# Turning the identity matrix in TensorE's waits, and moving slot and clear work on VectorE, in a cross-attention and mixture-of-experts kernel

## What is computed

```python
x = x + attention(layernorm(x), ctx, mask, W_q, W_k, W_v, W_o, b_o)
xf = layernorm(x)
probs = softmax(xf @ Wr)
topk_probs, topk_experts = top_k(probs, 2)
for e in range(8):
    gate = sum(where(topk_experts == e, topk_probs, 0))
    vals, idx = top_k(where(any(topk_experts == e), gate, -inf), 1120)
    h = relu(xf[idx] @ W1[e]) @ W2[e]
    y = y.at[idx].add(where(isfinite(vals), vals, 0)[:, None] * h)
return x + y
```

## Time and profile before

| | |
|---|---|
| median of 3 runs | 2058.97 us (2055.81 to 2060.05) |
| the profiled execution's own time | 2061.44 us |
| its span, first to last instruction | 2059.7 us |
| mean granted TensorE clock | 0.977 of full |
| busy: PE / DVE / ACT / POOL | 95% / 49% / 35% / 23% |
| chain that ended last: PE, of it L1714 | 69%, 64% |
| PE busy in the stretch 578.3 to 622.7 us | 20.07 of 44.40 us |

### The profile page before, as it was taken

One profiled execution on the slowest core, in us unless ns is written; L12 is line 12 of the kernel. 1 busy time (PEld: TensorE's weight loads), 2 busy tenths in 40 slices (PEclk: granted clock), 3 DMA queues, 4 the chain that ended last, 5 costly groups with the idle time before them and its releaser, 6 DMA issues.

```text
span 2059.7 us, 30182 instructions
## 1 busy us (share of the span) xinstructions
PE 1954.4 (95%) x11419; PEld 1733.6 (84%) x11419; DVE 1002.4 (49%) x2471; ACT 719.4 (35%) x1928; POOL 477.0 (23%) x560
## 2 busy tenths in 40 slices
PE   5799999999849999999999999999999999999997
PEld 4688888888638889989889888888998988889996
DVE  4678888887676353334133413432343353236221
ACT  4566776666414132123112311321132132115111
POOL 2445555455510021011001100111101011112101
PEclk9899999999959999999999999999999999999999
DMA  7011332211144144124112411341142144116102
GB/s 210 19 52 53 87 87 74 66 53 36 54 142 144 16 118 123 15 52 145 45 15 57 139 46 16 105 120 31 28 141 73 16 112 113 31 21 162 32 5 27
DMA packets 96316, 148.40 MB, mean 72 GB/s; under 512 B 8608, under 2 KB 50096, under 8 KB 96160
## 3 DMA queue, kind: packets, MB, share of 16 engines
q1 hardware_dynamic: 80288, 109.41, 16.9%
q0 software_dynamic: 15872, 36.71, 9.9%
HBM read 110.70 MB, written 35.39 MB: 71 GB/s over the span
## 4 chain that ended last, share of the span: by engine, by line
PE 69%; DVE 1%; issue 1%; POOL 0%; POOLq 0%; ACT 0%; DVEq 0%
PE psH L1714 33%; PE psY L1714 31%; PE psY L1753 2%; PE psX L1728 1%; PE psI L1776 1%; DVE w_lo L1129 0%; PE psI L1766 0%; POOL out_dram L1498 0%; POOLq L1410 0%; DVE hT_lo L1688 0%; PE psI L1782 0%; DVE moves L1564 0%; DVE onehot L1572 0%; DVE slot_tile L1649 0%; DVE ys L1647 0%
## 5 line engine op out<-in xcount | busy, mean ns | idle before, releaser
L1688 DVE SCALAR_TENSOR_TENSOR hT_lo<-psH,hT_hi 128x384 fp32r<-128x384 f32 (+1 forms) x384 | 210.0, 547 | 867.3 <-ACT hT_hi L1528 527.9
L1528 ACT ACTIVATE hT_hi<-psH 128x384 fp32r<-128x384 f32 (+1 forms) x384 | 185.4, 483 | 1063.3 <-PE psH L1714 1063.3
L1714 PE MATMUL psH<-xgT_hi,w_hi 128*128 128x256 f32 (+3 forms) x1536 | 477.7, 311 | 9.6 <-issue 8.8
L1714 PE MATMUL psH<-xgT_hi,w_lo 128*128 128x256 f32 (+3 forms) x1536 | 476.6, 310 | 2.1 <-issue 2.1
L1714 PE MATMUL psH<-xgT_lo,w_hi 128*128 128x256 f32 (+3 forms) x1536 | 475.3, 309 | 1.7 <-issue 1.7
L1714 PE MATMUL psY<-w_hi,hT_hi 128*128 128x512 f32 (+1 forms) x921 | 371.7, 404 | 0.0
L1714 PE MATMUL psY<-w_lo,hT_hi 128*128 128x512 f32 (+1 forms) x921 | 362.7, 394 | 1.1 <-issue 1.1
L1714 PE MATMUL psY<-w_hi,hT_lo 128*128 128x512 f32 (+1 forms) x921 | 362.3, 393 | 0.0
L1714 PEld LDWEIGHTS psH<-xgT_hi,w_hi 128*128 128x128 f32 x1536 | 291.5, 190 | 35.3 <-issue 18.5
L1714 PEld LDWEIGHTS psH<-xgT_lo,w_hi 128*128 128x128 f32 x1536 | 291.7, 190 | 14.9
L1714 PEld LDWEIGHTS psH<-xgT_hi,w_lo 128*128 128x128 f32 x1536 | 291.4, 190 | 4.1 <-issue 4.1
(11 more groups left out here) (229 smaller groups left out, 2870.2 us busy)
## 6 DMA issues: line engine op xcount, KB each, us to landing
stage<-in_L_ffn_W_dram SPq DMA_DIRECT2D x128, 512.0 KB, 4.5
x_sb<-in_x_dram SPq DMA_DIRECT2D x8, 896.0 KB, 5.6
x_res<-in_x_dram SPq DMA_DIRECT2D x8, 896.0 KB, 5.6
out_dram<-x_res SPq DMA_DIRECT2D x8, 896.0 KB, 4.8
xn_rows<-xn SPq DMA_DIRECT2D x8, 896.0 KB, 4.8
c_sb<-in_ctx_dram SPq DMA_DIRECT2D x8, 384.0 KB, 6.2
c_sb<-in_ctx_dram SPq DMA_DIRECT2D x32, 96.0 KB, 5.8
out_dram<-zrow SPq DMA_DIRECT2D x9, 256.0 KB, 4.2
```

The lines of the kernel that those rows point to most:

```text
L1528: h = nc.scalar.activation(hT[0][:, f % 2, 0:m], psH[f % 2][:, 0:m], ACT.Relu)
L1688: h = nc.vector.scalar_tensor_tensor(out=hT[1][:, f % 2, 0:m], in0=psH[f % 2][:, 0:m], scalar=0.0, in1=f32(hT[0][:, f % 2, 0:m]), op0=ALU. ...
L1714: mm = nc.tensor.matmul(out, stationary(a, c), moving(b, c), start=first and c == chunks[0] and j == 0, stop=last and c == chunks[-1] and ...
```

## The change

A helper `turn_over` transposes the 128x128 identity matrix into a PSUM bank that is free at the time. Nobody reads the result, and the turns wait for nothing and raise no semaphore. They are put ahead of TensorE's waits: 42 in the prologue, 16 after it, 25 in `PE_END`, 40 in the router and 80 at the start of the experts, 203 in all. On VectorE, `place(slice(1, E))` goes from behind `gid` to behind the gates, ahead of the first `h_lo`. The clears of the two `psH` banks go from behind it to the end of `early_slots`, ahead of the wait for the last early product.

```diff
+def turn_over(nc, T, bank, times):
+    for _ in range(times):
+        nc.tensor.transpose(bank[:, 0:128], T["ident"][:], T["ident"][:])
...
-PE_END = order("t-3 o-4 t-2 o-3 wo0 t-1 o-2 wo1 o-1 wo2 tt0 wo3 tt1 tt2 tt3 lg0 lt0")
+PE_END = order("t-3 o-4 t-2 o-3 wo0 t-1 o-2 wo1 o-1 x6 wo2 tt0 wo3 x10 tt1 x4 tt2 tt3 x5 lg0 lt0")
+IDLE = {("fc", 0): 22, ("fc", 2): 4, ("fx", 0): 7, ("fx", 2): 4, ("k", 0): 2, ("q", 0): 3}
...
+                    elif kind == "x":
+                        turn_over(nc, T, psS[1], i)
...
             for kind, i in PRO_ORDER:
                 if kind == "q":
                     pe.wait_ge(zeros, 6)
+                turn_over(nc, T, psS[1], IDLE.get((kind, i), 0))
                 proj(None, False, True, kind, i, 1)
+            turn_over(nc, T, psS[1], 16)
             iteration(0, False, True)
...
         def _(pe):
+            turn_over(nc, T, idle, 32)
             pe.wait_ge(consts, 5)
             pe.wait_ge(counts, 1)
             nc.tensor.matmul(ps[0:R, 0:E], T["ones_m"][:], cnt[:], start=True, stop=True).then_inc(counted, 1)
             positions(pe, nc, T, marks, placed)
+            turn_over(nc, T, idle, 8)
             pe.wait_ge(placed, 1)
...
                 for q in range(GROUPS):
                     slot_onehot(0, 0, q)
+                for bank in psH:
+                    nc.vector.memset(bank[:], 0.0)
                 dve.wait_ge(slot_mm, GROUPS)
                 nc.vector.tensor_copy(gid[0][:], psI[:, 0:CAPT]).then_inc(ids_ready, 1)
...
             early_slots()
-            place(slice(1, E))
-            for bank in (*psH, psY[BLK - 1]):
-                s = nc.vector.memset(bank[:], 0.0)
-            s.then_inc(cleared, 1)
+            nc.vector.memset(psY[BLK - 1][:], 0.0).then_inc(cleared, 1)
...
             then_gate(nc.vector.memset(T["vals"][:, :, :, 3], 1.0))
+            place(slice(1, E))
             for n in range(NBLOCKS):
...
+            turn_over(nc, T, psY[0], 16)
             for q in range(GROUPS):
                 early_product(q)
+            turn_over(nc, T, psY[0], 48)
             for c in range(DCH):
                 turn(0, c)
+                turn_over(nc, T, psY[0], 4)
             pe.wait_ge(cleared, 1)
             hidden(0, 0, True)
```

More of the change, by code:

```diff
@@ L1198, in router @@
         extra = sb("extra", [R, NBLK, E])
-        ps = ctx.enter_context(nc.psum_tensor("count_ps", [128, 512], F32))
+        ps, idle = [ctx.enter_context(nc.psum_tensor(n, [128, 512], F32)) for n in ("count_ps", "idle_ps")]
         iotas, consts, step, counted, counts = sem("iotas"), sem("consts"), sem("step"), sem("counted"), sem("counts")
```

## The result

The changed kernel takes **2073.5 us** (median of 6 runs, 2068.5 to 2077.9) against 2059.5 for the kernel before in the same session (6 runs, 2055.0 to 2065.0). The ratio is 1.0066, 95% interval 1.0043 to 1.0088: 0.66% or 13.6 us slower. The prediction was 2058.8, range 2052 to 2066.

What follows compares the result with a forecast made beforehand. PE, busy 95% of the span, was taken as the bound, so gains lay where it idles or its clock is low. Terms -1.5 - 0.7 + 2.0 = -0.2 us, put on the median: 2058.8 us, range 2052 to 2066.

Steps and rivals of the forecast that it cites:

- the sum: Whole kernel: prologue -1.5, start of first `output` -0.7, later clock +2.0, together -0.2 us; everything behind 622.7 us just shifts.
- Gathers, +1.0: Gathers after `gid`: SyncE's next 1 MB load starts some 4 us earlier, beside the third gather, delaying it 1.0 us.
- Chunks, -1.4: From 608.64 us to DVE's last `xgT_lo`: two transpose groups of 1.43 us are halved, saving 1.4 us.
- `place`, +3.2: Ahead of the first `h_lo`: the moved `place` lengthens DVE's chain 3.2 us, 1.9 absorbed; PE waits for `h_lo`.
- Prologue, -1.5: First loads and first pair: 22 turns delay transposes by 3.7 us net, but a higher clock saves more; net -1.5 us.
- Logits -2.4: End of attention: the 25 turns hold the clock up, so L776's 5.31 us nearly halves, saving 2.4 us.
- router +0.8: Router: PE idles again after 32 turns, its clock falls, and the 8 turns behind `positions` make it last; +0.8 us.
- `gid` 0: Early products up to `gid`: the `psH` clears (1.03 us) are hidden behind PE's eight groups; 0, bounds 0 and 0.5 us.
- Do turns count?: Premise that turns, being transposes, bring TensorE's clock up; the rival that they don't gave 2072 us, chance 8%.
- The clock behind the stall, +2.0: After PE's waits around the second `hidden`, the clock falls to 0.50; 2.4 less 0.4 gives +2.0 us.
- The rivals: Turns don't count, 2072 us, 8%; too late with load in the way, 2063.5, 15%; turns fill waits, 2053.1, 27%.
- The second: Rival: clock rises only after the first query product, third gather 2.8 us late, stall costs 3.05; 2063.5 us, chance 15%.

Runs made afterwards that it cites:

- `code_only`: The kernel before, with 203 identity transposes in a branch this data never enters, so the experts' TensorE code lies 406 instructions later; 2067.5 us, ratio 1.0058.
- `best_place`: The kernel before, with 99 identity transposes (198 instructions) in the branch this data never enters; 2051 us, ratio 0.9965.
- `no_first_turns`: The change's turns with before's DVE order and 24 never-run transposes, minus the 58 turns of the first loads and iteration 0; total time not given.
- `turns_only`: The changed kernel's turns with the kernel before's order on DVE (place and psH clears behind gid again); ratio 1.0057 to the kernel before.
- `worst_place`: The kernel before, with 69 identity transposes (138 instructions) in the branch this data never enters; 2074 us.

## Why the prediction was wrong, point by point

**The step that failed** is the last sentence of the sum: "Behind 622.7 PE is the bound to the end (95% busy by the page), and all of it just moves along." PE was the bound, but its code does not just move along. The change shifts all of the experts' code by 406 instructions, and that alone cost 12 us (`code_only`), nearly the whole 13.6. I had the sign of it in hand: the 8.32 us at the start I read as a jump whose code must arrive, and the "issue" rows at 619.19 too, but took their size for fixed. The 9.6 us that PE stood before products of `hidden` in the page of before, 8.8 of them "issue", said that such waits were worth a look everywhere.

**Gathers, +1.0 with bounds 0 and 2.8.** The mis-sized term: +4.3 (from -4.4 to -0.1 us). I took one gather and the first load behind it. In fact loads of two pairs start while all three gathers are under way, the later ones wait behind the earlier, and I had not thought of GpSimd's slower issue at all (+1.0 in the first two).

**Chunks, -1.4.** It did not happen, +0.7 instead (-0.1 to +0.6 us at the last `xgT_lo`): the landing was late, so the 48 turns ran out, PE stood for 4.25 us, and the four chunks with their turns went at 0.50.

**`place`, +3.2 of which 1.9 absorbed.** The chain was right, and PE did wait for `hT_lo`, 2.94 us. The price of the move came by another way, through the loads that it let go.

**Prologue, -1.5.** The trace showed -1.8 and the 22 turns where I had put them. But this one difference of two executions is not evidence. The saving did not come as I had it, either: the first query product took 2.71 us instead of 4.78, the second, named as a sign with 2.6, took 4.17 instead of 4.74; and without a single turn they took 2.67 and 3.52 in `best_place`. The first product of the logits starts at 570.55 before, and at 568.55, 566.03, 563.68, 568.24 and 567.95 in five kernels with the very same attention. With all turns of the change it is 565.0 to 568.9 in eight; without the first 58, 567.0 and 568.0. The first turns are worth nothing that can be measured (`no_first_turns`), and the execution that I read was itself nearly 4 us to the slow side there.

**Logits -2.4, router +0.8, `gid` 0.** The first two were right: 8 products in 3.17 us instead of 5.31; then -2.5 and +1.0. `gid` was not 0 but -1.1: the early products start 3.3 us earlier than before and `gid` 4.4, since they go faster at the full clock and DVE keeps up.

**Do turns count?** Yes. L783 runs at full clock behind the 25 turns, and the early products do behind the 16 turns (granted clock 0.99 from 590.6 to 594.0), where it was 0.50 before. The rule that I weighed against it (the Trainium skill, "TensorE: Matmul & The Clock Gate", part 4 on the PE-mode transpose) does not hold in this case. One reading of mine was too high: the transposes of tokens and context in the first of the earlier trace rows last 1.8 us, not more than 2.

**The clock behind the stall, +2.0.** It was low for 3.4 us, from 624.8 to 628.2, instead of the 6.8 that I had taken over: +1.2.

**The rivals.** None named the cause. The second ("too late, and the load is in the way", 2063.5) had the load, and for the gathers 2.8 us where 4.3 were measured.

In sum, at the changed kernel's place of the code: 12 us for the place (`code_only`), nothing for the turns (`turns_only` has the same ratio), and for the moves on DVE 2 us by the ratios of `turns_only` and the changed kernel, whose intervals overlap, or 5 by their traces from `gid` on. At the favourable place the same moves cost 7 to 9. Why less here is not shown; in both traces PE stands at n = 0 anyway (4.18 us in `turns_only`, 2.08 in the changed kernel).

## What to carry to other kernels

Adding instructions to an engine whose code is fetched during the run (here in 125 transfers), and that jumps far, shifts the code behind them, and the time can move (here from 0.35% under the kernel before to 0.73% over it) without any of the work having changed. So compare such a change with a control that has the same instructions where they never run, and look for waits put down to "issue" some 3 us behind jumps, or at a jump that follows close to another. An engine off the critical path sets when transfers start: before moving its work earlier, list the loads that this lets go and what is then on the queues; if the order is right otherwise, hold the loads with a wait instead.

## What the runs showed of the hardware that was not expected

- TensorE's code arrives during the run in transfers of 16.4 KB. A far jump takes 3.2 to 5.9 us; if from about 7 to some 45 instructions are left in the target's block, PE stands another 0.8 to 3.6 us in most cases, about 3 us later. Of the eight such cases counted for `worst_place` two did not show it (n = 7, where the count may be off by one, and n = 22, which is open). Targets at a block's start (252 to 255 left: n = 5, 6 and 22 in `code_only`, n = 8 and 9 in `best_place`) cost nothing.
- Where a jump comes about 1 us behind another (n = 10, 13, 19), PE runs out of products before the jump ends, by up to 0.8 us. If the block behind the first jump's target is late, the second jump starts 3.3 to 3.9 us behind the first, and the gap is 1.8 to 2.8 us.
- The issue of the first gather on GpSimd takes 1.24 us, and 1.97 while VectorE makes `w_lo` from two SBUF operands; beside `place`, which also reads two, it stays at 1.24.
- An attention of 560 us with nothing changed ended within 6.9 us in six kernels. A difference of 2 us at one point of two traces means nothing in this kernel.
